# Carrying the last expert pairs' rows to the first four tiles by 0/1 products on TensorE instead of through the scatter in device memory

## The chip, the cores and the metric

The kernel runs on one core of one Trainium2 chip. The metric is the device time of one launch in microseconds (us). Below, PE is TensorE, DVE is VectorE, ACT is ScalarE, POOL is GpSimd, and SP is SyncE, which here only issues DMAs (direct memory accesses). All five run at once, each through its own list of instructions in order, and meet at semaphores.

## The reference, cut to what matters

The program has two layers. Each multiplies the output of an attention-like mixer with a gate, the silu of a mixture of experts, and adds that to the residual. The change is at the seam between the experts of the first layer and the start of the second. The reference there:

```python
topk_w, topk_idx = jax.lax.top_k(scores, 8)            # 2048 tokens (4 x 512), 64 experts
...
dest = jnp.where(valid, slot_expert * CAP + pos, E * CAP)  # CAP = 64 rows for each expert
buf = jnp.zeros((E * CAP + 1, h)).at[dest].set(xf[slot_token])
xb = buf[:E * CAP].reshape(E, CAP, h)
hmid = silu(einsum(xb, w_gate)) * einsum(xb, w_up)
yb = einsum(hmid, w_down)                               # one row of 256 for each slot
slot_out = yb[dest] * topk_w
out = jnp.zeros((T, h)).at[slot_token].add(slot_out)    # sum of up to 8 rows for each token
...
x = x + s * silu(out)
xn = layernorm(x)                                       # then the second layer's attention
```

Only 64 x 64 = 4096 slots are kept, so each token's output is a sum of the rows of those of its eight experts that had room for it.

## The kernel before, in words

**Stages.** Stage 3 runs the 64 experts as 32 pairs (`PAIRS`), 128 slots for each pair. Stage 4 is the second layer's attention over 64 heads' turns; it begins with a prologue that finishes the first four tiles (`TPB` = 4 tiles of 128 tokens, one batch). A barrier, `stage_end`, stands between two stages: each engine adds to the semaphore `stage` and waits for all five.

**A pair in stage 3.** PE turns the 128 gathered rows (`expert_rows`, L976, three pairs ahead), multiplies by the gate and up weights (`expert_up`, L988, two ahead), runs two products whose result nobody reads (`keep_clock`, L968, ahead of the transpose), turns the hidden rows (`expert_turn`, L997, one ahead) and multiplies by the down weights (`expert_down`, L1005). ACT copies and applies silu between these. DVE forms the product of silu, up and the token's share (`h_product`, L1855) and copies the pair's 128 output rows from PSUM into one of four buffers `y0` (L1870). POOL scatters these rows into `z_d` in device memory (`scatter_rows`, L2322). `z_d` holds, for each tile of 128 tokens, 8 x 128 rows, one for each choice of each token; choices without a slot stay zero.

**Units.** Beside the pairs, 32 pieces of the second layer's weights are prepared: PE forms a low-rank product in bank `ps[7]` (`low_rank`, L1016 or L1024), DVE adds the raw weight (`add_low_rank`, L1847), ACT rounds to 16 bits (L1407), and DVE keeps the rest as a second 16-bit part (`low_part`, L1840). `UNITS_OF` says where: one at the `end` of each of the pairs 4 to 29, and one more in the middle (`mid`) of the pairs 12, 14, 16, 18, 20 and 22. A mid unit stands in PE's order ahead of the pair's transpose and waits until DVE has added the unit before it.

**The prologue of stage 4.** After the barrier, which POOL enters only when all 32 scatters have landed, SP loads the 1024 rows of each of tiles 1, 0, 3, 2 (1 MB each, L788). Tiles 1 and 3 are summed over the eight choices by PE, as products with the identity (`rows_summed`, L1051, eight for each tile); tiles 0 and 2 by DVE in three steps (`summed`, L1886 to L1890). ACT applies tanh (`half_gate`, L1450), in the order 0, 1, 3, 2, and DVE forms the residual and its statistics (`finish`, `spreads`, `scales`). Only after the last of the four tanhs does ACT take the square roots (L1455), normalise (L1461), and PE turns the rows (`turn_rows`, L1059), computes the router's logits (L1066) and starts the first head's projection (`project`, L1091). The rows of tiles 4 to 7 are loaded by SP (L791), half of them, and the other half is added by DMAs that POOL issues (`add_rows`, L2356, L2361); POOL also multiplies by the sine table for each head (L2344), behind these in its order.

## Times and profile before

| | us |
|---|---|
| median of 3 runs | 1121.68 |
| lowest, highest | 1120.18, 1124.24 |
| the profiled execution, its time | 1121.71 |
| its span in the trace | 1119.9 |

The span is what the trace covers, from the first to the last instruction; the execution's own time is 1.8 us more. PE is busy for 988 us of the span (88%), DVE for 854, ACT for 668 and POOL for 542. Stage 3 lies from about 130 to 237 us, the prologue of stage 4 from there to about 270 us.

### The profile page before, as it was taken

To read this page: it belongs to the slowest core of one execution; us is meant where nothing else is said; L and a number is where in the kernel's file an instruction comes from. 1 tells how busy PE (TensorE), PEld (TensorE's weight loads), DVE (VectorE), ACT (ScalarE), POOL (GpSimd) and SP (SyncE) were. 2 spreads that over 40 slices of the span, in tenths; PEclk is the share of its full clock that TensorE was granted. 3 is DMA by queue.
4 is the path that set the end of the run, shared out by engine and by line. 5 is a ranking of instruction groups with operands and counts; after the bars stand their busy time and mean duration, and the time that the engine had idled before them with its cause. 6 is when DMAs were issued, how large, how long until landed. Compare 5 with 4: busy or idle time off the path is not lost.

```text
span 1119.9 us, 22276 instructions
## 1 busy us (share of the span) xinstructions
PE 987.8 (88%) x6773; PEld 653.8 (58%) x6773; DVE 854.3 (76%) x2247; ACT 667.9 (60%) x1738; POOL 542.2 (48%) x532
## 2 busy tenths in 40 slices
PE   3966888956999999999999999999987899999984
PEld 2645533433566665676666657667654578885442
DVE  4788558846798679868678999999846877775677
ACT  1732434514768767867866667666635877775332
POOL 0478556512764565544444445444411345553774
PEclk9978989976999999999999999999988999999997
DMA  9979599979571565221111101210049345553443
GB/s 338 340 232 353 152 256 312 301 262 248 88 189 44 126 121 128 55 58 41 57 53 39 38 2 38 91 39 1 1 153 303 97 133 144 145 141 92 133 131 95
DMA packets 97023, 155.99 MB, mean 139 GB/s; under 512 B 12272, under 2 KB 67312, under 8 KB 94096
## 3 DMA queue, kind: packets, MB, share of 16 engines
q1 hardware_dynamic: 77184, 115.42, 31.9%
q0 software_dynamic: 19728, 39.21, 16.0%
q8 instruction: 56, 0.92, 0.3%
q14 instruction: 55, 0.45, 0.1%
HBM read 104.84 MB, written 45.02 MB: 134 GB/s over the span
## 4 chain that ended last, share of the span: by engine, by line
PE 56%; DVE 15%; ACT 9%; issue 6%; DVEq 4%; DMA 3%; POOL 3%; POOLq 2%; ACTq 1%; SPq 0%
PE ps L1091 9%; PE ps L1263 6%; PE ps L1155 5%; PE ps L1105 5%; PE ps L1143 4%; PE ps L1123 3%; PE ps L1209 3%; PE ps L1226 3%; ACT arena L1515 2%; PE ps L1281 2%; PE ps L905 2%; PE ps L988 1%; PE ps L1253 1%; PE ps L1133 1%; PE ps L1005 1%
## 5 line engine op out<-in xcount | busy, mean ns | idle before, releaser
L2344 POOL TENSOR_TENSOR arena<-arena 128x512 f32<-128x512 f32 x128 | 174.5, 1421 | 97.2 <-ACT arena L1492 97.1
L1091 PE MATMUL ps<-arena 128*128 128x512 f16 x768 | 178.5, 382 | 1.3 <-ACT arena L1492 1.3
L2349 POOL TENSOR_TENSOR arena<-arena 128x512 f32<-128x512 f32 x64 | 67.8, 1059 | 177.5 <-DVE arena L1994 177.5
L2386 POOL DMA_INDIRECT wvo<-xn_d,idx x79 | 75.9, 961 | 116.7 <-PE ps L1253 98.5
L1091 PEld LDWEIGHTS ps<-arena 128*128 128x128 f16 x768 | 75.3, 98 | 93.9 <-ACT arena L1492 3.5
L1515 ACT ACTIVATE arena<-arena 128x128 f32<-128x128 f32 x256 | 99.2, 390 | 38.7 <-DVEq L1989 38.7
L1491 ACT ACTIVATE arena<-ps 64x512 f32<-64x512 f32 x128 | 76.1, 595 | 52.7 <-DVE arena L1962 49.2
L1155 PE MATMUL ps<-wvo,arena 128*128 128x256 f16 x768 | 96.3, 277 | 5.6 <-DVE arena L2006 3.0
L1143 PE MATMUL ps<-arena 128*128 128x192 f32 (+1 forms) x512 | 94.3, 327 | 2.4 <-DVE arena L2000 2.4
L1962 DVE TENSOR_TENSOR arena<-ps,wvo 128x512 f32<-128x512 f32 x128 | 84.8, 684 | 14.7 <-PE ps L1091 14.7
L1105 PE MATMUL ps<-wvo,arena 128*128 128x512 f16 x384 | 93.0, 379 | 3.1 <-issue 1.6
L1155 PEld LDWEIGHTS ps<-wvo,arena 128*128 128x128 f16 x768 | 76.0, 100 | 26.2 <-DVE arena L2006 4.4
L1143 PEld LDWEIGHTS ps<-arena 128*128 128x128 f32 x512 | 82.2, 191 | 13.4 <-issue 10.8
L1972 DVE TENSOR_TENSOR arena<-arena 128x512 f32<-128x512 f32 x128 | 85.9, 712 | 3.3 <-POOL arena L2344 3.3
L1263 PE MATMUL ps<-arena,wvo 128*128 x474 | 84.5, 315 | 4.0 <-DVE arena L2191 4.0
L2391 POOL DMA_INDIRECT wvo<-y_d,row x64 | 63.7, 995 | 35.7 <-issue 18.6
L1123 PE MATMUL ps<-arena 128*64 128x128 f32 x1024 | 70.9, 281 | 7.3 <-DVE arena L1972 7.3
L1492 ACT ACTIVATE arena<-ps 64x512 f32<-64x512 f32 x128 | 75.4, 589 | 1.5
L1508 ACT ACTIVATE arena<-ps 128x512 f16<-128x512 f32 x64 | 38.2, 597 | 57.1 <-PE ps L1143 56.4
L1209 PE MATMUL ps<-arena 128*128 128x512 f16 (+1 forms) x288 | 64.3, 380 | 7.8 <-DVE arena L2180 6.9
L1123 PEld LDWEIGHTS ps<-arena 128*64 128x64 f32 x1024 | 55.6, 138 | 17.8 <-issue 16.5
L1986 DVE CUSTOM_DVE_ANT_0 arena<-ps,arena 128x128 f32<-128x128 f32 x256 | 58.6, 284 | 6.9 <-PE ps L1123 6.5
(295 smaller groups left out, 2199.0 us busy)
## 6 DMA issues: line engine op xcount, KB each, us to landing
arena<-wqk_d SPq DMA_DIRECT2D x16, 1024.0 KB, 5.8
arena<-in_wgu SPq DMA_DIRECT2D x32, 384.0 KB, 7.4
y_d<-wvo SPq DMA_DIRECT2D x79, 128.0 KB, 2.4
z_d<-wvo SPq DMA_DIRECT2D x8, 1024.0 KB, 4.3
z_d<-wvo SPq DMA_DIRECT2D x2, 4096.0 KB, 27.0
arena<-in_wdn SPq DMA_DIRECT2D x32, 192.0 KB, 10.8
arena<-z_d SPq DMA_DIRECT2D x12, 512.0 KB, 4.4
arena<-z_d POOLq DMA_DIRECT2D x12, 512.0 KB, 6.8
```

What stands on the lines that cost most here:

```text
L1091: last = pe.matmul(ps[s][:, :], wqk[gg][:, s * DC + c, w, hh * DH:(hh + 1) * DH], hx[bb][:, :, x, c * P:(c + 1) * P], start=(c == 0 and w ...
L1105: last = pe.matmul(values_bank(n, q)[:, :], hx[bb][:, q, x, c * P:(c + 1) * P], wvo16[:, UNITS + c * NG + g, w], start=(c == 0 and w == x) ...
L1123: last = pe.matmul(ps[3][side * WIN:(side + 1) * WIN, q * P:(q + 1) * P], qr[:, u, q * P + side * WIN:q * P + (side + 1) * WIN], kr[:, u, ...
L1143: last = pe.matmul(ps[7][:, k * P:k * P + n], vv[gg][:, k, hh * DH:(hh + 1) * DH], probs[:, k * KW + WIN:k * KW + WIN + n], start=(k == 0) ...
L1155: last = pe.matmul(output_bank(n, half)[:, q % 2 * D:(q % 2 + 1) * D], oT[gg][:, x, hh, q * P:(q + 1) * P], wvo16[:, 2 * g + hh // 2, w, h ...
L1209: last = pe.matmul(ps[2 * (c % 2) + g][0:rows, :], sgw16[:, 2 * d + g, w, c * P:c * P + rows], xb16[:, b % 2, :, x, d * P:(d + 1) * P], st ...
L1263: last = pe.matmul(ps[1 + j % 2][:, 0:2 * F1], xsT[:, j % 4, x, c * P:(c + 1) * P], w13[:, bass.ds(e, 1), w, c * 2 * F1:(c + 1) * 2 * F1]. ...
L1491: nc.scalar.activation(qk_s[0:64, s], ps[s][64:P, :], ACT.Copy)
L1515: nc.scalar.activation(pp[u][:, q], sm[:, q], ACT.Exp, bias=mn[:, q:q + 1], scale=-1.0, accum_out=rs[:, q:q + 1])
L1962: nc.vector.tensor_tensor(qk_c[:, s], ps[s][:, :], cos, ALU.mult).then_inc(cos_rd, 1)
L1972: nc.vector.tensor_tensor(dst, a, b, ALU.add).then_inc(rope_done, 1)
L2344: nc.gpsimd.tensor_tensor(qk_s[:, s], qk_s[:, s], sin, ALU.mult).then_inc(sin_done, 1)
```

## The change

What it does, in the order of the program:

- When the slots' rows are known (the tables at the end of stage 2), DVE also keeps, for the pairs 26 to 31 (`FROM` = 26, 28, 28, 28), each slot's token number, and adds 16384 to the scatter address of each row that belongs to tile 0 (pairs 26 and 27) or to tiles 0 to 3 (pairs 28 to 31). The scatter's bounds check drops these rows.
- In stage 3, DVE builds 0/1 matrices of 128 x 128 that say which slot of a pair belongs to which token of a tile: 2 in the turn of pair 23, and 16 in the turn of pair 28 (L1918 of the changed kernel). PE multiplies them with the `y0` buffers (`put_rows`, L1038): 18 products, 6 for tile 0 and 4 each for tiles 1, 2 and 3. 12 of these and the eight sums of tile 0 come before the barrier, the other 6 after it.
- The rows in `z_d` of tiles 0 to 3 are loaded in stage 3, when the scatters of the pairs ahead of `FROM` have landed, and PE sums all four tiles (L1076). DVE sums none.
- Units: mid units in the pairs 6, 8, ..., 24 (ten, six before), end units in the pairs 4 to 25 (to 29 before). `keep_clock` runs no more from the transpose of pair 27 on.
- POOL enters the barrier without waiting for the scatters; SP waits for them before it loads the rows of tiles 4 to 7. These loads now also wait until PE has summed tile 3.
- ACT's tanhs go in the order 0, 1, 2, 3.

```diff
+        FROM = (PAIRS - 6, PAIRS - 4, PAIRS - 4, PAIRS - 4)
...
         for j in range(PAIRS):
-            for place in ("mid",) * (j in (12, 14, 16, 18, 20, 22)) + ("end",) * (4 <= j < 30):
+            for place in ("mid",) * (j in range(6, 26, 2)) + ("end",) * (4 <= j < 26):
                 UNITS_OF[j, place] = len(UNITS_OF)
...
-        SUMMED = {0: (mix_done, 1), 2: (mix_done, 2), 1: (table0_mm, 5), 3: (table0_mm, 6)}
         def summed_at(t):
-            return SUMMED[t] if t < TPB else (mix_done, t - 1)
+            return (table0_mm, t + 5) if t < TPB else (mix_done, t - 3)
         def mix_of(t):
-            return ps[6 + t // 2][:, 0:D] if t in (1, 3) else mix[:, t % 2] if t < TPB else rows_of(t)[:, 0]
-        FIRST_FOUR = (0, 1, 3, 2)
+            return ps[(7, 2, 4, 5)[t]][:, 0:D] if t < TPB else rows_of(t)[:, 0]
...
@@ SP, end of stage 3
+            def put_down(n):
+                for u in range(4):
+                    sp.wait_ge(y0_out[u], 16 * len(range(u, n, 4)))
+            for t in range(TPB):
+                put_down(FROM[t])
+                upto(sp, y0_ps, (25, 27, 28, 28)[t])
+                if t >= 2:
+                    upto(sp, hm_ready, PAIRS - 1)
+                sp.dma_start(rows_of(t), z_d[t * K0 * P:(t + 1) * K0 * P, :]...).then_inc(yg_in[t], 16)
             stage_end(sp, 3)
             def load_rows(t):
-                if t < TPB:
-                    sp.dma_start(rows_of(t), z_d[...]).then_inc(yg_in[t], 16)
-                else:
-                    sp.wait_ge(*summed_at(t - TPB))
-                    ...
+                sp.wait_ge(*summed_at(max(t - TPB, TPB - 1)))
+                sp.dma_start(rows_of(t), z_d[t * K0 * P:t * K0 * P + K0 // 2 * P, :]...)
...
-            for t in (1, 0, 3, 2):
-                load_rows(t)
             sp.wait_ge(wqk_out, 16 * NG)
             load_group(0)
...
+            put_down(PAIRS)
             for t in range(TPB, 2 * TPB):
                 load_rows(t)
-            sp.wait_ge(*summed_at(3))
             load_group(1)
@@ PE
             def expert_turn(j):
                 upto(pe, hmT_rd, j - 1)
-                keep_clock(6, 2)
+                if j <= FROM[0]:
+                    keep_clock(6, 2)
...
+            def put_rows(j, t):
+                upto(pe, y0_rd, PAIRS - 1 if t == 3 else j)
+                pe.matmul(mix_of(t), kept_at[j][:, t], y0[:, j % 4], start=(j == FROM[t]), stop=False, skip_group_check=True)
...
                 expert_down(j)
                 for n in units_at((j, "end")):
                     low_rank(n)
-            stage_end(pe, 3)
+                if j == FROM[0] + 1:
+                    pe.wait_ge(chosen0, 5)
+                if j == PAIRS - 3:
+                    pe.wait_ge(chosen0, 6)
+                if j > FROM[0]:
+                    put_rows(j - 1, 0)
+                if j == PAIRS - 2:
+                    put_rows(j - 2, 1)
+                if j >= PAIRS - 2:
+                    put_rows(j - 1, 1)
+                if j == PAIRS - 1:
+                    upto(pe, y0_rd, j - 1)
+                    for k in range(FROM[2], j):
+                        put_rows(k, 2)
             def rows_summed(t):
                 pe.wait_ge(yg_in[t], 16)
                 for k in range(K0):
-                    last = pe.matmul(mix_of(t), ident[:, :], rows_of(t)[:, k], start=(k == 0), stop=(k == K0 - 1))
+                    last = pe.matmul(mix_of(t), ident[:, :], rows_of(t)[:, k], start=False, stop=(k == K0 - 1), skip_group_check=True)
                 last.then_inc(table0_mm, 1)
+            put_rows(PAIRS - 1, 0)
+            rows_summed(0)
+            stage_end(pe, 3)
+            put_rows(PAIRS - 1, 1)
+            put_rows(PAIRS - 1, 2)
+            for k in range(FROM[3], PAIRS):
+                put_rows(k, 3)
...
-            rows_summed(1)
-            rows_summed(3)
+            for t in range(1, TPB):
+                rows_summed(t)
@@ ACT
-            for t in FIRST_FOUR:
+            for t in range(TPB):
                 half_gate(t)
@@ DVE, tables at the end of stage 2
+            for a, b, tiles in ((FROM[0], FROM[1], 1), (FROM[1], PAIRS, TPB)):
+                nc.vector.tensor_scalar(rz[:, a - FROM[0]:b - FROM[0]], tile_no[:, a:b], float(tiles), float(NT * K0 * P), ALU.is_lt, ALU.mult)
             dve.drain()
+            nc.vector.tensor_tensor(row_f[:, FROM[0]:PAIRS], row_f[:, FROM[0]:PAIRS], rz[:, 0:PAIRS - FROM[0]], ALU.add)
+            dve.drain()
+            nc.vector.tensor_copy(rz[:, 0:PAIRS - FROM[0]], idx0[:, FROM[0]:PAIRS])
             nc.vector.scalar_tensor_tensor(put0[:, :], choice_no, float(P), row_f, ALU.mult, ALU.add)
@@ DVE, stage 3
-            for n in units_at((PAIRS - 1, "end")):
-                ...
+                if j in (FROM[0] - 3, PAIRS - 4):
+                    for k in range(FROM[0], FROM[1]) if j < FROM[0] else range(FROM[1], PAIRS):
+                        for t in range(1 if k < FROM[1] else TPB):
+                            nc.vector.tensor_scalar(kept_at[k][:, t], iota[:, :], rz[:, k - FROM[0]:k - FROM[0] + 1], -float(t * P), ALU.subtract, ALU.is_equal)
+                    dve.drain().then_inc(chosen0, 1)
             stage_end(dve, 3)
@@ DVE, stage 4
-            summed(0)
             finish(0)
             finish(1)
             spreads(slice(0, 2))
-            summed(2)
+            finish(2)
+            scales(1, slice(0, 2))
             finish(3)
-            scales(1, slice(0, 2))
-            finish(2)
             spreads(slice(2, TPB))
@@ POOL
-            for u in range(4):
-                pool.wait_ge(y0_out[u], 16 * PAIRS // 4)
             pool.sem_inc(stage, 1)
```

Three places show how this moves instructions. First TensorE from the end of pair 29 to its first sums of rows, before; L1005 is the down product (two for a pair), L968 `keep_clock`, L997 the transpose, L1024 a unit, L1051 a sum of rows:

```order
L1005 MATMUL ps<-arena 64x256
L1024 MATMUL ps<-arena 128x512 [waits lora_add]
L968 MATMUL ps<-ones_bf 128x512 [waits hmT_rd]
L968 MATMUL ps<-ones_bf 128x512
L997 MATMUL ps<-ident,arena 96x128 [waits hm_ready]
L1005 MATMUL ps<-arena 64x256 [waits y0_rd,hmT_rd]
L1005 MATMUL ps<-arena 64x256
L1005 MATMUL ps<-arena 64x256 [waits y0_rd,hmT_rd]
L1005 MATMUL ps<-arena 64x256
L1051 MATMUL ps<-arena,ident 128x256 [waits yg_in1,stage]
L1051 MATMUL ps<-arena,ident 128x256 x7
L1051 MATMUL ps<-arena,ident 128x256 [waits yg_in3]
```

And the same stretch after the change, where L1005 is the transpose, L1013 the down product, L1038 a 0/1 product (`put_rows`) and L1076 a sum of rows:

```order
L1038 MATMUL ps<-arena 128x256 [waits y0_rd,chosen0]
L1005 MATMUL ps<-ident,arena 96x128 [waits hm_ready,hmT_rd]
L1013 MATMUL ps<-arena 64x256 [waits y0_rd,hmT_rd]
L1013 MATMUL ps<-arena 64x256
L1038 MATMUL ps<-arena 128x256 [waits y0_rd] x3
L1013 MATMUL ps<-arena 64x256 [waits y0_rd,hmT_rd]
L1013 MATMUL ps<-arena 64x256
L1038 MATMUL ps<-arena 128x256 [waits y0_rd] x6
L1076 MATMUL ps<-arena,ident 128x256 [waits yg_in0]
L1076 MATMUL ps<-arena,ident 128x256 x7
L1038 MATMUL ps<-arena 128x256 [waits y0_rd,stage]
L1038 MATMUL ps<-arena 128x256 [waits y0_rd] x5
```

The unit and the clock keepers are gone from this stretch; 16 of the 18 0/1 products and tile 0's sums stand in it, and a wait for DVE's matrices (`chosen0`).

On DVE, the end of stage 3 before: h_product (L1855), the copy of the pair's rows (L1870), a unit's two parts (L1847, L1840), then the sum of tile 0 (L1886):

```order
L1855 SCALAR_TENSOR_TENSOR arena<-ps,arena 64x96
L1870 COPY arena<-ps 128x256 [waits y0_out1,y0_ps]
L1840 SCALAR_TENSOR_TENSOR arena<-arena,norm_up 128x512 [waits hi_done]
L1847 SCALAR_TENSOR_TENSOR arena<-ps,arena 128x512 [waits lora_mm]
L1870 COPY arena<-ps 128x256 [waits y0_out2,y0_ps]
L1840 SCALAR_TENSOR_TENSOR arena<-arena,norm_up 128x512 [waits hi_done]
L1870 COPY arena<-ps 128x256 [waits y0_out3,y0_ps]
L1840 SCALAR_TENSOR_TENSOR arena<-arena,norm_up 128x512 [waits hi_done]
L1886 TENSOR_TENSOR arena<-arena 128x1024 [waits yg_in0,stage]
```

The same after the change, from the copy of pair 28 (L1910) on; L1918 builds the matrices, L1895 is h_product, L1926 the first step of `finish`:

```order
L1910 COPY arena<-ps 128x256 [waits y0_out0,y0_ps]
L1918 TENSOR_SCALAR arena<-iota,rz 128x128 x16
L1895 SCALAR_TENSOR_TENSOR arena<-ps,arena 64x96 [waits hmT_ps,sg_ready]
L1895 SCALAR_TENSOR_TENSOR arena<-ps,arena 64x96
L1910 COPY arena<-ps 128x256 [waits y0_out1,y0_ps]
L1910 COPY arena<-ps 128x256 [waits y0_out2,y0_ps]
L1910 COPY arena<-ps 128x256 [waits y0_out3,y0_ps]
L1926 TENSOR_TENSOR arena<-ps,s_sb 128x256 [waits g_ready,stage]
```

No unit is left there, and the 16 builds stand between the copy of pair 28 and the h_product of pair 31.

In SP's list the loads of rows from `z_d` before, behind the last store of prepared weights (L782):

```order
L782 DMA wqk_d<-arena 128x2048 [waits lo_done] x4
L788 DMA arena<-z_d 128x8x256 [waits stage]
L788 DMA arena<-z_d 128x8x256 x3
L804 DMA arena<-wqk_d 128x2048 [waits wqk_out]
...
L791 DMA arena<-z_d 128x4x256 [waits mix_done]
```

And after the change, where L794 loads tiles 0 to 3 and L800 tiles 4 to 7:

```order
L782 DMA wqk_d<-arena 128x2048 [waits lo_done] x4
L794 DMA arena<-z_d 128x8x256 [waits y0_out3,y0_out2,y0_ps,y0_out1,y0_out0] x2
L794 DMA arena<-z_d 128x8x256 [waits y0_out3,y0_ps,y0_out2,hm_ready,y0_out1,y0_out0] x2
L813 DMA arena<-wqk_d 128x2048 [waits wqk_out,stage]
...
L800 DMA arena<-z_d 128x4x256 [waits y0_out3,y0_out2,table0_mm,y0_out1,y0_out0]
```

The first four loads have moved ahead of the barrier, and the wait of the first load of tiles 4 to 7 is now on PE's sums (`table0_mm`), not on DVE's first (`mix_done`).

## Rows read from the trace of the kernel before

**Rows 1.** Stretches: start:end us, length, busy of each engine, clock, DMA share, GB/s.

```profile
149.00:152.00 3.00, 0.88 (x4) 0.40 (x4) 1.03 (x2) 0.00 (x0) 0.00 (x0) 0.50 0.98 325
...
237.00:243.00 6.00, 0.00 (x0) 0.00 (x0) 0.00 (x0) 0.00 (x0) 0.00 (x0) 0.50 0.68 211
...
257.00:261.00 4.00, 0.00 (x0) 0.00 (x0) 3.39 (x10) 2.99 (x6) 1.41 (x1) 0.62 0.96 295
...
270.00:275.00 5.00, 5.00 (x14) 2.02 (x15) 2.53 (x15) 1.01 (x2) 2.21 (x2) 0.50 0.81 164
```

**Rows 2.** Timeline, pair 20 (with a mid unit) to pair 22: start, duration, instruction.

```profile
199.33 0.44 PE L976 MATMUL ps<-ident,arena 128*128 128x128 f32 x2
...
203.53 0.44 PE L976 MATMUL ps<-ident,arena 128*128 128x128 f32 x2
...
206.25 0.44 PE L976 MATMUL ps<-ident,arena 128*128 128x128 f32 x2
...
206.50 1.42 DVE L1840 SCALAR_TENSOR_TENSOR arena<-arena,norm_up 128x512 f16<-128x512 f32 x2
...
208.57 0.39 PE L1024 MATMUL ps<-arena 48*128 48x512 f16 x1 [1.09 <-DVE arena L1847]
```

**Rows 3.** Timeline, pair 26 and the last copy of stage 3.

```profile
218.60 0.44 PE L976 MATMUL ps<-ident,arena 128*128 128x128 f32 x2
...
219.77 0.61 PE L968 MATMUL ps<-ones_bf 128*128 128x512 bf16 x2
...
220.17 0.65 DVE L1855 SCALAR_TENSOR_TENSOR arena<-ps,arena 64x96 f32<-64x96 f32 x2
220.22 0.27 PE L997 MATMUL ps<-ident,arena 128*96 128x128 f32 x1
...
220.42 0.65 PE L1005 MATMUL ps<-arena 96*64 96x256 f32 x4
...
221.00 0.39 PE L1024 MATMUL ps<-arena 48*128 48x512 f16 x1
...
231.68 0.42 DVE L1870 COPY arena<-ps 128x256 f32<-128x256 f32 x1
```

**Rows 4.** Timeline, the prologue of stage 4, up to the second head's projection.

```profile
243.50 5.76 PE L1051 MATMUL ps<-arena,ident 128*128 128x256 f32 x16 [12.66 <-DMA arena<-z_d]
...
249.42 3.72 PE L1051 MATMUL ps<-arena,ident 128*128 128x256 f32 x16 [0.16 <-DMA arena<-z_d]
...
257.43 0.42 ACT L1450 ACTIVATE arena<-arena 128x256 f32<-128x256 f32 x1 [3.87 <-DVE arena L1890]
...
261.08 0.69 PE L1059 MATMUL ps<-ident,arena 128*128 128x128 f32 x2 [7.94 <-ACT arena L1463]
...
270.45 4.99 PE L1091 MATMUL ps<-arena 128*128 128x512 f16 x12
...
277.86 2.75 PE L1091 MATMUL ps<-arena 128*128 128x512 f16 x12
```

**Rows 5.** Timeline of four tensor_scalars of DVE in a later stage.

```profile
675.04 0.93 DVE L2052 TENSOR_SCALAR arena<-iota_bf,arena 128x80 f16<-128x80 bf16 x4
```

**Rows 6.** Groups by line and form, DVE: count | busy, mean ns | idle before.

```profile
L2052 DVE TENSOR_SCALAR arena<-iota_bf,arena 128x80 f16<-128x80 bf16 x64 | 29.8, 531 | 0.0
```

**Rows 7.** Timeline, POOL's first DMAs that add rows, and its first sine product.

```profile
258.77 1.41 POOL L2356 DMA_DIRECT2D arena<-z_d  x1 [24.60 <-DMA arena<-z_d]
...
270.38 0.91 POOL L2361 DMA_DIRECT2D arena<-arena  x1 [10.21 <-DMA arena<-z_d]
...
275.33 1.27 POOL L2344 TENSOR_TENSOR arena<-arena 128x512 f32<-128x512 f32 x1 [2.74 <-ACT arena L1492]
```

**Rows 8.** The loads of half a tile's rows (SP, L791), all twelve.

```profile
L791 SPq DMA_DIRECT2D arena<-z_d x12: 368/383/1834, 249.0 to 428.0; - x12
...
DMA to landing us min/median/max: 3.9/4.4/10.2
```

**Rows 9.** Timeline, DVE's second late tile in stage 2.

```profile
115.47 0.79 DVE L680 TENSOR_TENSOR arena<-arena 128x256 f32<-128x256 f32 x1 [1.47 <-ACT arena L1376]
```

More of the change, by code:

```diff
@@ L398, in build @@
         wqk16 = R3.take(P, 2 * UNITS, 2, 512, dt=F16)
+        R3.at = 512 + 2 * UNITS * 512
+        kept_at = {j: R3.take(P, TPB, P) for j in range(PAIRS - 4, PAIRS)}
         R3.at = 0
@@ L413, in build @@
         xg = R3.take(P, XGBUF, D + E0)
+        kept_at.update({j: R3.take(P, 1, P) for j in range(FROM[0], PAIRS - 4)})
         assert R3.at <= at_w - WBUF // 2 * (WGU + WDN)
@@ L491, in build @@
         hx = [R6.take(P, TPB, 2, 2 * D, dt=F16) for _ in range(2)]
-        yg_of = [yg[:, 0], yg[:, 1], flat(hx_f[1].rearrange("p a b c d -> p (a b c) d")).rearrange("p (k d) -> p k d", k=K0),
-                 wqk_f[1].rearrange("p (k d) -> p k d", k=K0)]
+        yg_of = [wqk_f[1].rearrange("p (k d) -> p k d", k=K0), flat(hx_f[1].rearrange("p a b c d -> p (a b c) d")).rearrange("p (k d) -> p k d", k=K0),
+                 yg[:, 0], yg[:, 1]]
         R7 = Region()
@@ L782, in _ @@
                 sp.dma_start(wqk_d[g], wqk_parts[:, g]).then_inc(wqk_out, 16)
+            def put_down(n):
[6 more added lines that the diff above has]
+                    upto(sp, hm_ready, PAIRS - 1)
+                sp.dma_start(rows_of(t), z_d[t * K0 * P:(t + 1) * K0 * P, :].rearrange("(k p) d -> p k d", p=P)).then_inc(yg_in[t], 16)
             stage_end(sp, 3)
             def load_rows(t):
-                if t < TPB:
-                    sp.dma_start(rows_of(t), z_d[t * K0 * P:(t + 1) * K0 * P, :].rearrange("(k p) d -> p k d", p=P)).then_inc(yg_in[t], 16)
-                else:
-                    sp.wait_ge(*summed_at(t - TPB))
-                    sp.dma_start(rows_of(t), z_d[t * K0 * P:t * K0 * P + K0 // 2 * P, :].rearrange("(k p) d -> p k d", p=P)).then_inc(yg_in[t % TPB], 16)
+                sp.wait_ge(*summed_at(max(t - TPB, TPB - 1)))
+                sp.dma_start(rows_of(t), z_d[t * K0 * P:t * K0 * P + K0 // 2 * P, :].rearrange("(k p) d -> p k d", p=P)).then_inc(yg_in[t % TPB], 16)
             def store_tile(t):
@@ L1874, in _ @@
                     low_part(n)
-            for n in units_at((PAIRS - 1, "end")):
-                add_low_rank(n)
-                low_part(n - 1)
-                low_part(n)
-            stage_end(dve, 3)
-            def summed(t):
-                u = t % 2
-                a = rows_of(t)
-                dve.wait_ge(yg_in[t], 16)
-                nc.vector.tensor_tensor(a[:, 0:4], a[:, 0:4], a[:, 4:8], ALU.add)
-                dve.drain()
-                nc.vector.tensor_tensor(a[:, 0:2], a[:, 0:2], a[:, 2:4], ALU.add)
-                dve.drain()
-                nc.vector.tensor_tensor(mix[:, u], a[:, 0], a[:, 1], ALU.add).then_inc(mix_done, 1)
+                if j in (FROM[0] - 3, PAIRS - 4):
[3 more added lines that the diff above has]
+                    dve.drain().then_inc(chosen0, 1)
+            stage_end(dve, 3)
             def finish(t):
                 u = t % 2
-                seen(dve, g_ready, FIRST_FOUR.index(t) if t < TPB else t)
+                seen(dve, g_ready, t)
                 nc.vector.tensor_tensor(mix[:, u], mix_of(t), s_sb[:, t], ALU.mult)
```

## The prediction, made before the changed kernel was run

> **What bounds the kernel now.** I read the table of stretches first. From 237 to 243 us no engine computes, the clock stands at its lower level (0.50, 1.2 of 2.4 GHz) and DMAs move [rows 1]: the seam after stage 3 is a wait for memory. The timeline then gives its pieces. DVE's last copy of a pair's rows ends at 232.1 [rows 3], PE's first sum of rows starts at 243.50 after 12.66 us of idleness that a load from `z_d` ends [rows 4]: 11.4 us pass for the last scatter, the barrier and a load of 1 MB. The order of ACT then decides. Its last tanh (L1450, tile 2) starts at 257.43 [rows 4], the square roots stand behind it, and 3.65 us later PE turns the first rows (261.08); the first projection starts at 270.45, and everything in stage 4 hangs on it. So the number to follow is the start of the last tanh: 257.43, 25.3 us after DVE's last copy of stage 3. Last I read a pair of stage 3 with a mid unit and one without. Without one, PE goes from the first transpose to the next in 2.72 us (203.53 to 206.25) and is never late for DVE; with one, the two pairs 20 and 21 take 6.92 (199.33 to 206.25), and the mid unit of pair 22 waits 1.09 us for DVE [rows 2]. There DVE is the bound.
>
> **Part 1: four more mid units.** A mid unit costs 6.92 - 2 x 2.72 = 1.48 us [rows 2]. Pairs 6, 8, 10 and 24 get one, the unit's work itself being the same wherever it stands: 4 x 1.48 = 5.9 us later at pair 26. Bounds: 0 if DVE had the time for them, 5.9 if it hasn't; I take 5.9, since the row with 1.09 us of waiting is of the same work. The two matrices built in the turn of pair 23 stand on DVE between a unit's parts and the sum for which the mid unit of pair 24 waits, so they count: 2 x 0.2 plus the drain, 0.5 us (their price is in part 3). Pair 26's first transpose moves from 218.60 [rows 3] to 225.0.
>
> **Part 2: pairs 26 to 28.** Removed in each: the end unit, from 221.00 to the next pair, 0.32, and the two clock keepers, 0.45 from their start to the transpose's (219.77 to 220.22) [rows 3]. A pair takes 2.72 - 0.77 = 1.95. With the first 0/1 product in pair 27 (0.43, below) and 0.2 for DVE's backlog of unit parts, the down product of pair 28 ends at 225.0 + 5.85 + 0.43 + 0.2 = 231.5, and its copy (0.42 [rows 3]) at 232.0.
>
> **Part 3: 16 builds on DVE.** They follow this copy, and the h_product of pair 31 is queued behind them, as are the copies of pairs 29 to 31; PE waits for both. The trace has no such operation. The nearest is a tensor_scalar with scalars read from memory over 80 columns: four in 0.93 us, 0.23 each at most, a little less from start to start [rows 5]; mine has one such scalar and 128 columns of 32 bits. I take 0.20. The lower bound is 0.14 (a third off, if the two scalars of that row cost what my one doesn't), the upper the mean of that group, 0.53 [rows 6], which is far over the timeline's 0.23 and tells that something blocks some of them. So 3.2 us, between 2.2 and 8.5. With the drain they end at 235.3.
>
> The Trainium skill ("SBUF — State Buffer", SBUF: two separate sides) says that VectorE and GpSimd share a pair of ports under an exclusive lock, for VectorE's 2-port modes among others, and the loser blocks for the whole instruction. POOL scatters pair 28 in these 3 us, and its issues of DMAs are spans of about 1 us (0.91 and 1.41 [rows 7]), so by that rule the builds would take some 4.2, and the sum below would be 1 us more; the 0.53 against 0.23 agrees with such a rule but doesn't prove it here. "VectorE: DVE Perf Modes" (Mode 2×_2P) says on the other side that fp32 tensor_scalar between SBUF operands runs at two results a cycle. The sum by this would be up to 1 us less. They cancel about, and neither enters.
>
> **Part 4: PE's chain from there.** A 128x256 fp32 product: eight in 3.72 us, of which 0.3 is the last one's end (the trace shows 16 instructions, two for each) [rows 4]; 0.43 each at the full clock. Both kinds of product have this shape. After the builds: the product of pair 28 ends at 235.8; h_product of pair 31 (0.65 [rows 3]) at 235.95; transpose (0.2, from 220.22 to 220.42) 236.2; down product of pair 30 (0.58, from 220.42 to 221.00 [rows 3]) 236.8; 3 products 238.1; the last down product 238.7; 5 + 1 products 241.3; tile 0's 8 sums 244.7; barrier 0.4: 245.1. Behind it 6 products and 24 sums, 30 x 0.43 = 12.9, and 0.3 for the end: 258.3. Tile 3's tanh starts at 258.35, against 257.43: +0.9 us. In short, 11.4 us of waiting for memory and DVE's sums have turned into 48 products in a row (20.6 us). What comes between the last copy and the last tanh shrinks from 25.3 to about 19, and what comes before grows by about 7.
>
> **Part 5: what hides, and what is late next.** The loads of tiles 0 to 3 leave the path: tile 0's starts once SP has sent the last wqk_d store, whose unit now ends at pair 27 (about 230), so 11 us ahead of its use at 241.3, and before the last scatter, the barrier and a load of 1 MB took 11.4 together [rows 3, 4]. Tiles 2 and 3 wait for h_product of pair 31 (236), 15 us ahead of their use. If a load came late, the delay would count in full. DVE's sums of tiles 0 and 2 go, but they end no wait any longer. The table work at the end of stage 2 (four more small operations and two drains, about 0.9 us) hides: DVE's second late tile waits 1.47 us for ACT [rows 9]. Late next is POOL. The first load of tiles 4 to 7 used to be issued at 249.0 [rows 8] and had landed at 258.77, when POOL began to add (L2356); POOL waited 10.21 us for that add and was free for the sine at about 272.6, 2.7 us ahead of need (275.33) [rows 7]. Now the load goes at 258.1, into an empty queue: 4.4 us by the median, not the 9.8 it took [rows 8]. It lands at 262.5, the add is issued, is complete by the same 11.6 us at 274.1, and POOL's two further DMAs (2.2 us until 272.6 before, from 270.38) end at 276.3. The sine is needed at 275.33 + 0.9 = 276.2. So 0.1; I take 0.5 for contention with 3 more halves of rows in the same time.
>
> **The sum.** +0.9 + 0.5 = +1.4 us on the profiled execution's 1121.71: 1123.1. The median of the runs is 1121.68, so the same number holds for it. Nothing else changes in the 850 us behind, which shift as one.
>
> **The rivals.** 0.3% of 1121.7 is 3.4 us, about what a measurement of this kernel can tell from no change; the limits are 1118.3 and 1125.1.
>
> A, the forecast: 1123.1, by itself between 1120 and 1126 (each of the 16 builds 0.14 to 0.28, some contention). Chance 0.45.
>
> B, the early mid units are free. From 149 to 152 us PE is busy for only 0.88 of 3 us [rows 1], waiting for memory, and if later pairs are just on time for their gathers, units would fill gaps. Against: the pairs without a mid unit go at 2.72 and show no such gap [rows 2]. Three of the four units gone from the cost: 1123.1 - 4.4 = 1118.7; with builds at 0.14 1117.7. Chance 0.16, two thirds of it under 1118.3.
>
> C, the clock. Before, it falls after the sums (0.62 from 257 to 261) and is 0.50 until 275 [rows 1]; the first projection then takes 4.99 us for what takes 2.75 at the full level [rows 4]. Now PE sums until 258.3 and is idle 3.65 us instead of 7.94. If the clock stays up: -2.3, and up to 0.5 on the turned rows. For it: the shorter gap. Against: from 149 to 152 us it stands at 0.50 with PE busy for 0.88 of the 3 us [rows 1], so gaps of that size are enough at times. And POOL's sine, which A has just on time, would then eat most of it. 1121, within the band. Chance 0.11.
>
> D, slower: tile 4's rows are late. They are asked for 9 us later than before, and POOL's order puts the sine of head 0 behind the add's landing. If the load takes 9.8 as before (three more loads, the weights of the second group and stores share the queues), the add lands at 279.5, POOL is free at 281.7, and the first head's scores wait 5.5 us: 1128.1. It decides from the point where the add lands after 274. Chance 0.19.
>
> E, slower: the wait of about 2 us for the matrices, with no clock keepers, lets the clock fall in the last pairs, or POOL's scatters block the builds. Products at the lower level take 0.86, and six of them cost 2.6: 1125.7. Chance 0.09.
>
> Faster by over 0.3%: two thirds of B, a little of A and C, 0.19. Slower: most of D (0.16), half of E (0.05) and A's edge (0.05), 0.26 in all. Within: 0.55. The range must hold B's middle and D's: 1117.7 to 1128.0.
>
> **What would show it.** Right: pair 26's first transpose near 225; no wait of PE's sums for `z_d`; the 16 builds about 3.2 us long with PE waiting for them some 2 us ahead of the product of pair 28; 30 products at 0.43 behind the barrier; the last tanh at 258 to 259; POOL's first sine at 276 to 277 and its wait for the add about 10 us. Wrong: pair 26 at 219 to 221 (B); a clock of 1.0 from 258 to 275 (C); POOL's sine well over 1 us after ACT's swap (D); products at 0.86 before the barrier (E). If the last tanh comes before 254, parts 1 or 3 are mis-sized.

## The result, and the profile after

The changed kernel took 1124.7 us (median of 22 runs, 1120.75 to 1129.17) where the kernel before took 1121.5 beside it (22 runs): a ratio of 1.0029, with a 95% interval of 1.0020 to 1.0039. It is 3.2 us slower: clear of the noise, since the interval leaves out 1, but just inside what the prediction called no change (3.4 us), and in its range. The profiled execution took 1126.37 us, its span 1124.6, 1.7 us over the median; a second profile, below, lies nearer to it. Three of all the runs used here (two of the kernel with two builds later, one of the last set) stood in a second, slower state of the chip, and the ratios leave them out. "Turn n" means the point at which PE starts the first transpose in the turn of pair n.

The end of the units, in PE's timeline of the kernel after (start, duration, instruction, and in brackets the idle time before it and what ended it). It answers to [rows 2]:

```profile
217.88 0.44 PE L983 MATMUL ps<-ident,arena 128*128 128x128 f32 x2
218.25 0.87 PE L995 MATMUL ps<-arena 128*64 128x192 f32 x8
220.82 0.61 PE L1032 MATMUL ps<-arena 48*128 48x512 f16 x1 [1.70 <-DVE arena L1887]
221.36 1.03 PE L975 MATMUL ps<-ones_bf 128*128 128x512 bf16 x2
...
224.74 1.55 PE L995 MATMUL ps<-arena 128*64 128x192 f32 x8
...
228.30 0.44 PE L983 MATMUL ps<-ident,arena 128*128 128x128 f32 x2
```

PE waits 1.70 us for the sum on which the mid unit of pair 24 depends, not 1.09 as in [rows 2]. Then everything on PE takes longer: the gate and up products 1.55 us for 0.87, the two clock keepers 1.03 for 0.60. Turns 24 and 25 take 10.4 us (217.88 to 228.30) where a pair of turns with a mid unit takes 6.92. The stretches of the same profile name the reason (start:end, length, busy time of PE, PEld, DVE, ACT and POOL, granted clock, DMA share, GB/s):

```profile
219.00:222.00 3.00, 1.30 (x5) 0.43 (x4) 2.71 (x7) 0.25 (x1) 2.42 (x2) 0.75 0.95 294
222.00:225.00 3.00, 3.00 (x11) 0.94 (x11) 1.45 (x4) 1.65 (x4) 0.03 (x1) 0.50 1.02 429
225.00:227.00 2.00, 2.00 (x10) 0.85 (x9) 0.75 (x3) 0.48 (x2) 0.98 (x1) 0.50 1.00 406
...
229.00:236.00 7.00, 7.00 (x55) 3.67 (x51) 6.58 (x17) 3.04 (x10) 3.46 (x3) 1.00 0.41 160
...
239.00:242.00 3.00, 2.80 (x12) 1.67 (x12) 1.38 (x4) 0.27 (x1) 0.98 (x1) 0.83 0.99 345
242.00:246.00 4.00, 4.00 (x16) 2.38 (x15) 0.42 (x1) 0.00 (x0) 1.71 (x2) 0.70 0.57 165
...
270.00:275.00 5.00, 3.12 (x17) 3.04 (x16) 2.08 (x5) 3.83 (x9) 0.30 (x1) 0.50 1.06 355
```

The clock fell to its lower level (0.50, 1.2 of 2.4 GHz) at the end of the idle time of 1.70 us: in stretches of 1 us it is 1.00 up to 220, 0.76 from 220 to 221, and 0.50 from 221 to 227 although PE is busy throughout. It fell once more, to 0.50 from 241 to 244, some 2 us after PE's second such wait had ended, and as before in the turning of the rows. What DVE did ahead of the first wait, and then in the last pairs:

```profile
218.14 1.41 DVE L1880 SCALAR_TENSOR_TENSOR arena<-arena,norm_up 128x512 f16<-128x512 f32 x2
219.47 0.47 DVE L1918 TENSOR_SCALAR arena<-iota,rz 128x128 f32<-128x128 f32 x2
220.07 0.69 DVE L1887 SCALAR_TENSOR_TENSOR arena<-ps,arena 128x512 f32<-128x512 f32 x1
...
235.03 0.42 DVE L1910 COPY arena<-ps 128x256 f32<-128x256 f32 x1
235.48 3.23 DVE L1918 TENSOR_SCALAR arena<-iota,rz 128x128 f32<-128x128 f32 x16
238.90 0.65 DVE L1895 SCALAR_TENSOR_TENSOR arena<-ps,arena 64x96 f32<-64x96 f32 x2 [0.19 <-issue]
```

Two builds stand between the units' parts and the sum (219.47, 0.47 us for both, and the drain: the sum starts 0.60 us after the first build). The 16 others are one block of 3.23 us, 0.20 each. PE's chain from there, with the tanh of the fourth tile and POOL's work, which answer to [rows 4, 7]:

```profile
238.79 0.70 PE L1038 MATMUL ps<-arena 128*128 128x256 f32 x2 [1.69 <-DVEq L1919]
...
246.85 3.62 PE L1076 MATMUL ps<-arena,ident 128*128 128x256 f32 x16
250.72 2.83 PE L1038 MATMUL ps<-arena 128*128 128x256 f32 x12 [0.26 <-PEq L192]
253.39 10.52 PE L1076 MATMUL ps<-arena,ident 128*128 128x256 f32 x48
...
263.95 0.38 ACT L1485 ACTIVATE arena<-ps 128x256 f32<-128x256 f32 x1 [3.07 <-PE ps L1076]
...
276.96 5.20 PE L1126 MATMUL ps<-arena 128*128 128x512 f16 x12
...
279.28 0.91 POOL L2387 DMA_DIRECT2D arena<-arena  x1 [8.98 <-DMA arena<-z_d]
279.87 1.62 POOL L2382 DMA_DIRECT2D arena<-z_d  x1
281.85 1.26 POOL L2370 TENSOR_TENSOR arena<-arena 128x512 f32<-128x512 f32 x1 [0.36 <-ACT arena L1527]
```

No sum waits for a load from `z_d` any more. POOL is free 0.4 us ahead of the sine product. The last copy of stage 3 ends at 244.48, and the last tanh follows 19.5 us later (25.3 before). But that copy itself is 12.4 us later than before, so the projection starts 6.5 us later in this execution.

### The profile page after: what moved, and what is told of

It reads as the page before. It is cut to its first block, busy times and chain, and to the rows that moved or that the text cites. A ratio compares the mean times of both kernels' runs of the same rounds, so it can differ in the third digit from the quotient of the medians.

```text
span 1124.6 us, 22427 instructions
## 1 busy us (share of the span) xinstructions
PE 1004.7 (89%) x6831; PEld 665.8 (59%) x6831; DVE 854.8 (76%) x2263; ACT 667.5 (59%) x1738; POOL 543.1 (48%) x532
## 4 chain that ended last, share of the span: by engine, by line
PE 58%; DVE 16%; ACT 9%; issue 6%; DVEq 4%; POOL 2%; DMA 2%; ACTq 1%; POOLq 1%; SPq 0%; PEldq 0%; PEld 0%
PE ps L1126 9%; PE ps L1298 6%; PE ps L1190 5%; PE ps L1140 5%; PE ps L1178 4%; PE ps L1158 3%; PE ps L1244 3%; PE ps L1261 3%; ACT arena L1550 3%; PE ps L912 2%; PE ps L1316 2%; PE ps L1013 1%; PE ps L1288 1%; PE ps L1168 1%; PE ps L995 1%
```

## The experiments

Twelve sets of runs were made in four lots, each lot beside runs of the kernel before. In the second lot (the kernels before and after once more, and the two under "Later builds and keepers") the kernel before takes 1123.2 us (31 runs); the others ran on three further chips where it takes 1150.8, 1154.1 and 1154.1 (35, 16 and 17 runs). Ratios are to the runs of before in the same lot. Landmarks are compared as distances within a profile, since the times up to turn 6 differ by some us from one execution to the next (153.5 to 160.9).

**Units table alone.** The kernel before with the changed table:

```diff
-            for place in ("mid",) * (j in (12, 14, 16, 18, 20, 22)) + ("end",) * (4 <= j < 30):
+            for place in ("mid",) * (j in range(6, 26, 2)) + ("end",) * (4 <= j < 26):
```

> The kernel before with one edit: the units' table of the changed kernel (mid units in pairs 6 to 24, end units in pairs 4 to 25). Theory U (each further mid unit costs 1.48 us because DVE has no time for it, and the units' table is the largest term of the change's loss): four mid units cost 5.9 us, four end units gone from pairs 26 to 29 give back 4 x 0.32 = 1.3; so about 4.6 us slower than before, 1126 against 1121.5, and the first transpose of pair 26 at about 224.5. Rival S (the mid units are nearly free, and the loss sits in the seam: builds, products, later loads): within 1 us of before.

From turn 6 to turn 26 it takes 67.94 us (158.13 to 226.07), where before took 62.44 (156.16 to 218.60): the four mid units cost 5.5 us. Without the end units the last pairs go at 2.4 us, and the first projection comes 116.50 us after turn 6 (114.29 before): +2.2 is left. The distances agree with the theory for the mid units, but the time contradicts it: 1147.94, ratio 0.9972 (0.9950 to 0.9994), faster by 2.9 us where 4.6 slower was expected. Turn 6 to projection is no source of a gain in this profile, so the gain lies outside, or other executions of before have clock falls that this one hasn't. Neither was shown, and this stays open. It shows what a difference of 2 us in the time is worth here.

**Two pairs kept, no block of builds in the way.** `FROM = (PAIRS - 2,) * 4`, the old table, 8 builds after the last copy, keepers in all turns and 12 more at the end.

> The changed kernel with 0/1 products for the pairs 30 and 31 alone (8 instead of 18), built after the last copy, the units' table of the kernel before, and the clock keepers in every pair, with twelve more clock-keeping products while the matrices are built. Theory U: nothing is later than before up to the last copy (232.1), 8 builds and 8 products follow, and the four sums go one after another from about 239, so the last tanh starts near 253 against 257.4 before and 264 in the profile after: about 4 us faster than before, 1117.5. Rival S: the seam costs as much as after, so near 1121.5 or slower.

Ratio 1.0016 (0.9989 to 1.0044): the gain of 4 us didn't come. PE's timeline of it:

```profile
177.83 0.39 PE L1030 MATMUL ps<-arena 48*128 48x512 f16 x1 [3.73 <-DVE arena L1871]
178.15 0.60 PE L974 MATMUL ps<-ones_bf 128*128 128x512 bf16 x2
178.59 0.38 PE L1003 MATMUL ps<-ident,arena 128*96 128x128 f32 x1
178.90 1.12 PE L1011 MATMUL ps<-arena 96*64 96x256 f32 x4
...
242.31 3.72 PE L1036 MATMUL ps<-arena 128*128 128x256 f32 x16 [0.86 <-issue]
249.12 5.41 PE L1060 MATMUL ps<-arena,ident 128*128 128x256 f32 x16 [3.09 <-DMA arena<-z_d]
254.79 10.60 PE L1060 MATMUL ps<-arena,ident 128*128 128x256 f32 x48 [0.26 <-PEq L192]
```

The lower rows show why: with two pairs kept the rows of tile 0 still arrive last (a wait of 3.09 us for `z_d`), and PE then sums all four tiles. Last copy to last tanh is 25.4 us, as before (25.3). So two pairs don't cover the waiting for memory, and the four to six of the changed kernel do (three were not tried). The upper rows are a stall in turn 12: ACT stands idle for 2.45 us and DVE for 3.53, for which the trace shows no cause, and behind it the same products take 1.12 us for 0.65. Turn 6 to turn 26 is 70.2 us there (62.4 before). Whether other executions have this stall is not known; the profiled one took 1152.77 us, with a median of 1153.19. It has the pattern of pair 24: PE idle, then the clock at half.

**Clock keepers in every turn**, on the changed kernel:

```diff
-                if j <= FROM[0]:
-                    keep_clock(6, 2)
+                keep_clock(6, 2)
```

> The changed kernel with the clock keepers in every pair, as before. In the trace of the changed kernel the clock is at its lower level from about 241 to 245 us, where 3 products took 2.47 us and a down product 1.12. Theory U with C (waiting for the 16 builds without clock keepers makes the clock fall there): the keepers fill part of the wait, the tail is about 2.5 us shorter where the clock fell, less the 0.45 each that two or three of them add: median 1 to 2 us under 1124.7. Rival K0 (the wait of 1.7 us is what matters, and keepers ahead of it change nothing): 1124.7 or up to 1 us more.

Ratio 1.0022 (0.9999 to 1.0045), so no gain shows. The first fall stays (PE waits 1.70 us, turn 24 to 26 takes 10.5 us: these turns had their keepers anyway). PE's idle time ahead of the 16 builds' first product is 1.16 us for 1.69, and the clock stays at 1.00 from 230 to 260. But so it did in the second profile of the unchanged kernel, below, which has no keepers there and stood idle for 1.70 us: the second fall comes in some executions only. The keepers have a price as well: turn 26 to the last tanh takes 35.2 us here and 34.1 there.

**The two builds two turns later**, behind the last mid unit:

```diff
-                if j in (FROM[0] - 3, PAIRS - 4):
+                if j in (FROM[0] - 1, PAIRS - 4):
```

> The changed kernel with the two matrices for pairs 26 and 27 built in the turn of pair 25 in place of pair 23. In the trace of the changed kernel PE waits 1.70 us ahead of the mid unit of pair 24 (1.09 at the earlier ones) and the clock is at its lower level from about 221 to 227 us. Theory C (these builds lengthen the gap and so let the clock fall, 3 us of the loss): PE's wait there is 1.1 us, the clock stays up, and the median is 2 to 3.5 us under 1124.7. Rival (the builds cost only their own time, 0.5 us, and the clock falls by chance): 1124.2, and the clock falls near there in some profiles all the same.

```profile
218.50 0.44 PE L983 MATMUL ps<-ident,arena 128*128 128x128 f32 x2
...
220.83 0.39 PE L1032 MATMUL ps<-arena 48*128 48x512 f16 x1 [1.09 <-DVE arena L1887]
...
225.41 0.44 PE L983 MATMUL ps<-ident,arena 128*128 128x128 f32 x2
```

Turn 24 to 26 takes 6.91 us (218.50 to 225.41), PE waits 1.09 us and the clock is 1.00 from 200 to 260. In the profile 3.5 us are gone; the two builds cost that much, for 0.6 us of DVE's time. The time agrees: ratio 0.9991 (0.9969 to 1.0014), and the median is 3.5 us under that of the kernel with keepers in every turn, in the same lot, though the two intervals just overlap.

**The kernel before against itself.**

> The kernel before, unchanged, timed against itself, so that the others of this call have a profile of before on their own chip. Theory (clock falls and stalls of single executions make a noise of some us, the ratio of two kernels is no better known than about 0.3%): ratio 1.000, within 0.997 to 1.003; turn 6 to turn 26 in 62.4 us, the first projection 144 us after the first transposes of pair 3 or so (270 us on its own clock), and the extra 28 us of the other chip, if it is that chip again, behind 900 us. Rival (something depends on where or when a kernel stands in the rounds): a ratio outside 0.997 to 1.003.

Ratio 0.999 (0.9976 to 1.0004). Turn 6 to the projection takes 115.59 us (114.29 in the first profile; turn 15 took 1.6 us more, at half clock, behind a wait of 1.02 us).

**The changed kernel again.**

> The changed kernel, unchanged, on the chip of the other kernels of this call. Theory (the clock falls at pair 24 each time, since the two builds in the turn of pair 23 lengthen a wait of PE from 1.09 to 1.70 us): turn 24 to turn 26 takes 10.4 us again, the first projection comes 5 to 7 us later than that of before in its profile, ratio about 1.003 (0.9 to 4 us). Rival (the fall was one of that single execution): turn 24 to 26 in 7.0 us, the last tanh about 3 us earlier, at 259 to 261.

1124.13 us, ratio 1.0010 (0.9989 to 1.0030). PE's timeline:

```profile
219.05 0.39 PE L1032 MATMUL ps<-arena 48*128 48x512 f16 x1 [1.70 <-DVE arena L1887]
219.37 0.96 PE L975 MATMUL ps<-ones_bf 128*128 128x512 bf16 x2
...
226.70 0.44 PE L983 MATMUL ps<-ident,arena 128*128 128x128 f32 x2
...
237.19 0.70 PE L1038 MATMUL ps<-arena 128*128 128x256 f32 x2 [1.70 <-DVEq L1919]
...
238.89 1.56 PE L1038 MATMUL ps<-arena 128*128 128x256 f32 x6
...
250.20 10.52 PE L1076 MATMUL ps<-arena,ident 128*128 128x256 f32 x48
```

The same wait of 1.70 us, the same fall, 10.6 us for the two turns. The second wait (1.70) brings no fall here: six instructions of products take 1.56 us (2.47 in the first profile). Last tanh at 260.76, projection at 273.74, 118.64 us after turn 6: 4.35 more than the kernel before.

**The keepers ahead of the mid unit** in that one turn, the builds where they were:

```diff
+                if j == FROM[0] - 2:
+                    upto(pe, hmT_rd, j)
+                    keep_clock(6, 2)
                 for n in units_at((j, "mid")):
                     low_rank(n)
```

(and none in the next `expert_turn`).

> After, with the two clock keepers of one turn, that of pair 24, ahead of the mid unit and its wait instead of behind it; the two builds stay where they are. Theory (it is the 1.70 us in which PE computes nothing that lets the clock fall, not the builds as such): PE waits 1.2 us, the clock stays at its upper level, turn 24 to turn 26 takes 7.0 to 7.5 us where after took 10.4 and 10.6. Rival (the builds delay something else, or any delay of that turn brings the fall): 10 us again, with the clock at half.

```profile
221.46 0.61 PE L975 MATMUL ps<-ones_bf 128*128 128x512 bf16 x2
223.22 0.39 PE L1032 MATMUL ps<-arena 48*128 48x512 f16 x1 [1.16 <-issue]
223.54 0.31 PE L1005 MATMUL ps<-ident,arena 128*96 128x128 f32 x1
...
227.54 0.44 PE L983 MATMUL ps<-ident,arena 128*128 128x128 f32 x2
```

PE now stands idle for 1.16 us, and nothing is slow behind it: turn 24 to 26 takes 7.26 us. On DVE the builds and the sum start as far behind turn 24 as in the changed kernel (1.59 and 2.19 us). So it is PE's idle time, not the builds as such, that costs the clock, and the rival is refuted, in one profile (one run of 1148.93 us, no ratio). Behind the wait for the 16 builds, 1.69 us here too, the clock did fall (0.50 from 241 to 243).

**The 16 builds twice.** A second pass writes the same matrices again. The edit also puts a drain ahead of each pass, that of the two builds in pair 23's turn too, and there PE waits 1.89 us for 1.70.

> After, with the 16 builds of pairs 28 to 31 made twice over (the second pass writes the same). Theory (the builds stand on the path at about 0.20 each): another 3.2 to 3.4 us between the copy of pair 28 and the last tanh, which took 28.5 and 26.9 us in two profiles of after, so 30 to 31.7; a longer idle time of PE may cost 2 to 3 us more in clock. Rival (a part of the builds is hidden beside PE's work): 1.5 us or less.

```profile
237.61 6.53 DVE L1920 TENSOR_SCALAR arena<-iota,rz 128x128 f32<-128x128 f32 x32
...
244.22 1.22 PE L1038 MATMUL ps<-arena 128*128 128x256 f32 x2 [5.07 <-DVEq L1921]
...
246.64 2.93 PE L1038 MATMUL ps<-arena 128*128 128x256 f32 x6
```

32 builds take 6.53 us, 0.204 each, and PE's wait grows from 1.69 to 5.07: all 3.3 us of the second pass stand on the path. The rival is refuted. Copy of pair 28 to last tanh is 32.5 us (26.9 in the second profile of the unchanged kernel); the other 2.3 is the clock again, products at half speed behind the wait. (One run, 1162.75 us, no ratio.)

**Later builds and keepers; and the same with the 16 builds split.** The first has the edits of the two kernels above (two builds later, keepers everywhere); the second moreover makes the matrices when they are needed, 8 behind the copy of pair 28, 4 behind that of pair 29 and 4 behind that of pair 30 (shown in part: PE also gets two more waits):

```diff
+                BUILDS = {FROM[0] - 1: [(k, 0) for k in range(FROM[0], FROM[1])], PAIRS - 4: [(k, t) for t in range(2) for k in range(FROM[1], PAIRS)],
+                          PAIRS - 3: [(k, 2) for k in range(FROM[1], PAIRS)], PAIRS - 2: [(k, 3) for k in range(FROM[1], PAIRS)]}
```

> After, with two of the three edits: the two builds in the turn of pair 25, and clock keepers in all pairs; the 16 builds in one piece. Theory: turn 24 to 26 in 6.9 us (10.4 in after), the clock at its upper level to the projection's turn; turn 26 to last tanh 34.5 to 35.5 us; ratio to before 0.998 to 1.000, about 3.5 us under after. Rival (one keeps the clock fall whatever stands there): 10 us for the two pairs and a ratio like after's.

> After, with three edits: the two builds of pairs 26 and 27 one turn after the last mid unit (that of pair 25), clock keepers in all pairs, and the 16 builds of pairs 28 to 31 not in one piece behind the copy of pair 28 but 8 there, 4 behind the copy of pair 29 and 4 behind that of pair 30. Theory (PE's 1.7 us of idleness ahead of the product of pair 28 is the builds', 3.2 us in one piece, while half would do): beside the 3.5 us at pair 24, another 1.0 to 1.7 us off copy 31 to the last tanh; turn 26 to the last tanh in 33 us where after took 35.65; ratio to before 0.996 to 0.999. Rival (the chain of DVE copies and PE sums behind is what counts, the idle time comes out elsewhere): turn 26 to the last tanh as in the next kernel, within 0.3 us.

1122.56 us, ratio 1.0004 (0.9984 to 1.0024), and 1121.27 us, ratio 0.9990 (0.9974 to 1.0007). The clock is 1.00 from 158 to 250 in both. Turn 26 to last tanh takes 35.2 us (221.96 to 257.14) and 34.0 (222.76 to 256.72): splitting gives 1.2 us, as expected, though the 33 us of the expectation were not reached. Turn 6 to projection is 116.2 in both (the second lost 1.4 us to a half clock in turn 6).

**Half of the sums on DVE.** In the split kernel PE is never idle from 236 to 256 except for 0.26 us at the barrier, while DVE has nothing to do for 6.35 and 4.47 us there. So DVE adds rows 4 to 7 of each tile to rows 0 to 3, and PE sums four (shown in part, without the calls of `halved`).

```diff
-                pe.wait_ge(yg_in[t], 16)
-                for k in range(K0):
+                pe.wait_ge(chosen0, 9 + t)
+                for k in range(K0 // 2):
...
+            def halved(t):
+                a = rows_of(t)
+                dve.wait_ge(yg_in[t], 16)
+                nc.vector.tensor_tensor(a[:, 0:4], a[:, 0:4], a[:, 4:8], ALU.add)
+                dve.drain().then_inc(chosen0, 1)
```

> The kernel with the split builds, and VectorE adds the upper four of each tile's eight rows to the lower four as soon as they have landed (one sum of 1024 columns, 1.23 us where the kernel before has it), so that PE has 4 products of a tile to sum and not 8. Theory (the last tanh is the end of PE's chain of 48 products and sums at 0.44, and the rows of the fourth tile, issued at 235.65 and 11.3 us under way in the split kernel's profile, land at 247.0): tile 0's sums end 1.7 us sooner; the chain would be 7 us shorter, the last rows bound it at 247.0 + 1.3 + 1.8; last tanh at 250 to 251.5 where it was 256.7, the first projection at 263.5 to 265, ratio to before 0.992 to 0.996. Rival (what follows the tanh, VectorE's chain and the ACT table load, takes the gain back, or the loads land later when they meet others): last tanh early but the projection no more than 3 us earlier, ratio 0.997 to 1.0.

```profile
248.02 5.57 PE L1076 MATMUL ps<-arena,ident 128*128 128x256 f32 x24
...
250.29 1.23 DVE L1927 TENSOR_TENSOR arena<-arena 128x1024 f32<-128x1024 f32 x1 [0.69 <-DMA arena<-z_d]
...
253.63 0.38 ACT L1486 ACTIVATE arena<-ps 128x256 f32<-128x256 f32 x1 [1.53 <-PE ps L1076]
...
257.48 0.60 ACT L1497 ACTIVATE s_sb<-x_sb,st 128x256 f32<-128x256 f32 x1 [1.94 <-DVE st L1964]
```

1144.18 us (11 runs) against 1154.09, ratio 0.9921 (0.9893 to 0.9949). Turn 26 to last tanh falls from 34.0 to 27.3 us. The last rows now bound the sums (DVE waits 0.69 us for them), and 1.7 of the 6.7 us are given back: from the last tanh to the projection 14.65 us pass where it was 12.98, since ACT waits 1.94 us for DVE, which is behind with its statistics. Turn 26 to the projection is 41.9 us, against 46.9 in the split kernel and 51.9 in the kernel before.

From turn 6 to the projection it is 109.87 us, 4.4 less than in the kernel before. The ratio says 9, so it ran once more, unchanged.

> The kernel with VectorE's half sums, unchanged, a second time, since its ratio of 0.9921 (some 9 us) is twice what its profile accounts for: from turn 6 to the first projection it took 109.9 us where the kernel before takes 114.3, 4.4 us less, and behind the projection nothing was changed. Theory (the seam's 4.4 us is all; the rest is that chip's, on which the units table alone also ran 5 us faster than its own distances say): ratio 0.995 to 0.998, and turn 6 to projection again at 109 to 111 us. Rival (starting the second layer earlier, or the new units table, saves something that these distances don't hold): ratio 0.990 to 0.994 again.

1148.15 us (12 runs) against 1154.05, ratio 0.9947 (0.9921 to 0.9973): 6 us, between the theory and the rival, whose ranges both overlap the interval. Turn 6 to projection is 113.11 in this profile, outside the expectation: turn 6 itself ran at half clock (4.97 us for 3.32), and the fourth tile's rows landed late: DVE waited 2.31 us for them (0.69 in the first profile), and so PE 1.54 for DVE:

```profile
252.15 3.65 PE L1076 MATMUL ps<-arena,ident 128*128 128x256 f32 x16
257.34 1.99 PE L1076 MATMUL ps<-arena,ident 128*128 128x256 f32 x8 [1.54 <-DVEq L1928]
```

Both intervals lie below 1, and by either this kernel is faster than the one before. The seam accounts for 4.4 us by the first profile and 1.2 by the second. How much of the rest lies elsewhere and how much is those chips is open, since no profile of the kernel before was taken on them. With the sums halved, the landing of the last rows (0.69 and 2.31 us of waiting for DVE) is what limits next.

## Why the prediction was right or wrong

The forecast of no change held, at +3.2 us where +1.4 was forecast. That it held is partly luck: one step failed by 3 us, and the median shows less than the distances in the profiles do. By its steps:

- **Part 1, the mid units**: 1.48 each, 5.9 forecast, 5.5 measured by the units table alone. Rival B (they are free) is refuted.
- **Part 1, the two builds in pair 23's turn**: the step that failed. It counted them as 0.5 us of DVE's time on a wait. They cost 3.5 (10.4 against 6.91 with the builds elsewhere), since the longer wait takes PE's clock down; a term of 3.0 us for this was missing from the sum. Turn 26 was at 228.30 and 226.70 in the two profiles, not 225.0. The prediction knew this mechanism, and placed it (rival E) only at the wait behind the 16 builds.
- **Part 2**: 1.95 to 2.0 a turn without unit and keepers (228.30 to 230.30), as forecast; with a product it is 2.53. Turn 26 to the end of pair 28's copy took 7.15 us, forecast 7.0.
- **Part 3**: 16 builds in 3.23 us, forecast 3.2, though a scatter of POOL (236.24) stood beside them. The Trainium skill ("SBUF — State Buffer", SBUF: two separate sides) describes an exclusive lock on the ports that VectorE and GpSimd share. The 4.2 us that the prediction worked out by it don't show here; the trace decides for 0.20 each.
- **Part 4**: the chain of products at 0.44. Copy of pair 28 to last tanh took 26.9 us in the second profile, forecast 26.35; in the first 28.5, with rival E's fall behind the 1.69 us wait. E is thus right in some executions: of four profiles with a wait of 1.69 or 1.70 us for the 16 builds two have the fall.
- **Part 5**: POOL's wait for the add was 8.98 us, and it was ready 0.4 us ahead of the sine product. The 0.5 us put in for contention isn't there, and rival D is refuted: projection to sine takes 4.88 or 4.89 us in all profiles, before and after.
- **Rival C**: refuted. The clock is up until 268, then at 0.50 from 270; the projection's 12 products take 5.20 us, and 4.60 in the second profile (4.99 and 4.57 in the two of the kernel before).

From turn 6 on the second profile of the changed kernel takes 4.35 us more than the kernel before: 0.9 forecast up to the last tanh, 3.0 for the clock at pair 24, and 0.45 of small terms. The first takes 7.1 more: the further 2.7 are 1.6 for the second fall and 1.3 for a half clock in turn 6, which the first profile has (4.58 us for 3.32) and the second hasn't, less 0.2 of small terms. Against the second profile of the kernel before, with its own fall, the 4.35 are 3.05. That the median rose by only 3.2 and, on the other lot, by 1.1 us (-1.2 to +3.4) goes with turn 6 coming 0.6 to 1.3 us earlier in the changed kernel's profiles of these two sets (155.60 and 155.10, against 156.16 and 156.45). Why it does was not found: the loads that turn 4 and 5 wait for land at other times, and no edit touches them, unless through the added table work at the end of stage 2. Behind the projection little differs: 849.5 and 849.2 us before, 847.6 and 849.0 after.

So the change did what it says, 11.4 us of waiting for memory have gone, and they went into three things: 5.5 us of mid units, 3.5 us of clock, and a chain of 48 products on PE while DVE stood idle. The last two can be had back, as the kernel with the half sums shows.

## What to carry to other kernels

When an instruction is put ahead of a wait, don't price it at its own time alone: look at how long the waiting PE then stands idle, and whether idle times of that length are followed by slow products elsewhere in the trace. An extra 0.6 us cost 3.5 here, and moving two clock keepers in front of the wait saved nearly all of it (3.2, in one profile). And when a wait for memory is replaced by work on one engine, look at once which engine is idle beside it, and halve the work there.

## What the runs showed of the hardware

- PE's waits of 1.02 to 1.09 us for a unit's sum (86 in fourteen profiles) were followed by a fall of the clock once. The wait at pair 24 brought it down in four profiles of four (1.70 us in three, 1.89 in the kernel with the builds twice), and the wait of 1.69 or 1.70 us for the 16 builds in two of four (the first profile of the changed kernel and the one with the keepers ahead of the mid unit; not in the second profile of the changed kernel, nor with the two builds later). With keepers in every turn this wait was 1.16 us, and no fall followed in two profiles.
- The fall doesn't coincide with the wait. It came 0.3 us before PE went on in the first profile (an estimate from 0.76 in the stretch from 220 to 221, with PE going on at 220.82), and some 2 us after that at the 16 builds. Once down behind pair 24, the clock stood at 0.50 from 221 to 227 although PE was busy throughout, and behind the 16 builds from 241 to 244.
- The same kernel took 1121.5 and 1123.2 us in two sets of runs and 1150.8 to 1154.1 in the others. The difference isn't at the change: behind the projection 847 to 849 us pass in the six profiles of the first two sets and 870 to 878 in the eight others. From 950 to 1000 us PE is busy throughout in all of them, with 142 to 146 GB/s moved by DMAs; from 1050 to 1100 it is 121 to 124 GB/s in those six and 73 to 97 in the eight. Why is open. Ratios within a lot aren't touched by it, but absolute times are.
